# Expert up products with the weights stationary: weights copied inside SBUF for each slot, the turns of the product rows left out

## The reference, cut to what matters

```
D, F, E = 128, 512, 8                       # channels, hidden width, experts
logits = x @ gate_w
mult, sel = _sparse_mixer_routing(logits)   # two experts for each token, and their weights
w = jnp.sum(mult[:, :, None] * (sel[:, :, None] == jnp.arange(E)[None, None, :]), axis=1)
h = jax.nn.silu(jnp.einsum('th,ehf->etf', x, w1)) * jnp.einsum('th,ehf->etf', x, w3)
out = jnp.einsum('etf,efh,te->th', h, w2, w)
```

## Time and profile before

| what | us |
|---|---|
| median of 3 runs (1183.71 to 1185.48) | 1183.82 |
| the profiled execution | 1184.85 |
| its span, from the first to the last instruction | 1183.1 |
| TensorE busy (82% of the span) | 964.7 |
| DVE busy (68%) | 808.8 |
| ScalarE busy (43%) | 510.1 |
| GpSimd busy (36%) | 431.0 |
| DMA queue of SP, share of 16 DMA engines over the span | 13.5% |

### The profile page before, as it was taken

How to read it: one execution, slowest core, us unless ns; L and a number is a source line. 1 busy time by engine, 2 the same in 40 slices (tenths; PEclk the granted TensorE clock), 3 DMA queues, 4 the chain that set the end, 5 groups by cost and what they waited for, 6 DMA issues and landing times. The chain is left out here.

```text
span 1183.1 us, 17682 instructions
## 1 busy us (share of the span) xinstructions
PE 964.7 (82%) x6003; PEld 495.9 (42%) x6003; DVE 808.8 (68%) x1504; ACT 510.1 (43%) x1048; POOL 431.0 (36%) x506
## 2 busy tenths in 40 slices
PE   5497899999999999769867964599983994399993
PEld 3232322322222332346644423366651664156662
DVE  6886989999888770388987976533347786733335
ACT  5344577687877677432012111133334431123333
POOL 3320110011011111236853871266642785146661
PEclk9598999999999899979978996699996997689997
DMA  5843500000000000332101201011112210111114
GB/s 126 176 93 55 108 2 1 1 2 2 1 2 1 2 3 1 137 94 70 40 0 32 68 9 36 15 44 42 43 35 80 63 37 1 38 32 43 43 43 121
DMA packets 50205, 51.47 MB, mean 44 GB/s; under 512 B 7668, under 2 KB 39804, under 8 KB 50108
## 3 DMA queue, kind: packets, MB, share of 16 engines
q1 hardware_dynamic: 45128, 40.11, 13.5%
q0 software_dynamic: 4992, 10.23, 3.2%
HBM read 33.22 MB, written 16.91 MB: 42 GB/s over the span
## 5 line engine op out<-in xcount | busy, mean ns | idle before, releaser
L724 DVE TENSOR_REDUCE mpart<-ps 128x2 f32<-128x1024 f32 (+3 forms) x320 | 324.8, 1061 | 47.6 <-PE ps L775 29.2
L852 ACT ACTIVATE arena<-ps 128x512 f32<-128x512 f32 (+3 forms) x640 | 291.7, 543 | 132.1 <-PE ps L792 131.6
L792 PE MATMUL ps<-arena 51*128 51x512 bf16 (+3 forms) x640 | 175.2, 357 | 13.2 <-DMA arena<-mrow 6.3
L806 PE MATMUL ps<-arena,w 128*32 128x512 f32 (+3 forms) x1280 | 153.4, 551 | 2.8 <-ACT arena L852 2.1
L775 PE MATMUL ps<-arena 51*128 51x512 bf16 (+3 forms) x640 | 141.5, 361 | 12.1 <-DVE mpart L724 5.8
L694 POOL TENSOR_SCALAR_AFFINE_SELECT arena<-arena 128x512 f32<-128x512 f32 x64 | 40.6, 635 | 299.3 <-ACT arena L852 219.9
L1689 ACT ACTIVATE arena<-ps 128x512 f32<-128x512 f32 x78 | 46.6, 597 | 219.4 <-PE ps L1752 161.0
L1096 POOL TENSOR_TENSOR arena<-arena 128x512 f32<-128x512 f32 x96 | 121.0, 1272 | 46.2 <-DVE arena L1148 45.8
L1599 DVE COPY arena<-ps 128x128 f32<-128x128 f32 x78 | 22.8, 292 | 150.6 <-PE ps L1742 137.5
L792 PEld LDWEIGHTS ps<-arena 51*128 51x128 bf16 x640 | 49.3, 94 | 167.5 <-ACT arena L852 130.4
L1148 DVE TENSOR_TENSOR_SCAN arena<-ps,arena 128x512 f32<-128x512 f32 x96 | 118.3, 1253 | 0.4 <-POOL arena L1101 0.4
(11 more groups left out here) (265 smaller groups left out, 1440.5 us busy)
## 6 DMA issues: line engine op xcount, KB each, us to landing
w<-in_w SPq DMA_DIRECT2D x2, 2048.0 KB, 11.0
arena<-results SPq DMA_DIRECT2D x16, 256.0 KB, 5.1
arena<-q_stack SPq DMA_DIRECT2D x8, 384.0 KB
arena<-k_stack SPq DMA_DIRECT2D x8, 384.0 KB
arena<-g_v SPq DMA_DIRECT2D x9, 256.0 KB, 4.5
arena<-r_v SPq DMA_DIRECT2D x9, 256.0 KB, 3.6
arena<-l_v SPq DMA_DIRECT2D x9, 256.0 KB, 3.6
tokens<-arena SPq DMA_DIRECT2D x8, 256.0 KB, 2.4
```

The costliest lines, as they stand in the source:

```text
L724: nc.vector.tensor_reduce(out=mpart[:, 2 * pl:2 * pl + 2, t, kc], in_=ps[:, bank:bank + 2, 0:width], axis=AX.X, op=ALU.max).then_inc(ring_ ...
L792: nc.tensor.matmul(ps[:, n % ST, off:CH], rows(Ks, j % 2, 2 * g + j // 2, kt * P, (kt + 1) * P), rows(Qs, j % 2, 2 * g + j // 2, c * CH + ...
L806: ins = nc.tensor.matmul(ps[32 * j:32 * j + 32, O, off:CH], vg[kt // (NT // 2)][:, kt % (NT // 2), g * GH + j, :], probs[:, u % 2, j, off: ...
L852: nc.scalar.activation(probs[:, n % 2, j[0], off:CH], ps[:, (GH * n + j[0]) % ST, off:CH], ACT.Exp, scale=float(HD) ** -0.5).then_inc(exp_ ...
```

## The change

The up products change their sides: the expert's w1 and w3 become the stationary operand, in pieces of 128 hidden channels, and the turned tokens the moving one, 128 columns. Eight products take the place of two. Their result has the hidden channels on the partitions already, so the four turns on TensorE and the copy on ScalarE go, with the buffer `hid` and two semaphores; DVE's multiplication writes `hidT` itself. The down product of a slot moves one pass of the loop earlier.

The stationary pieces are read from a fixed place, `w13` (two buffers of 128 x 2 x 512). SP fills it: for each slot it reads the expert into a register, waits until the up products two slots back are done, and issues two DMAs of 128 x 512 words from `w1` and `w3` in SBUF to `w13` in SBUF. TensorE waits for both.

```
+            w13 = take(2 * 2 * F).rearrange("p (b u f) -> p b u f", b=2, u=2)
 ...
                             dve.wait_ge(silu_out, i + 1)
                             if i >= 2:
-                                dve.wait_ge(hid_turned, i - 1)
-                            nc.vector.tensor_tensor(hid[:, i % 2, :], ps[:, 2 + i % 2, :], act_a[:, i % 2, :],
-                                                    ALU.mult).then_inc(hid_ready, 1)
-                        s = i - 2
+                                dve.wait_ge(down_ready, i - 1)
+                            nc.vector.tensor_tensor(hidT[:, i % 2, :, :].rearrange("p f t -> p (f t)"), ps[:, 2 + i % 2, :],
+                                                    act_a[:, i % 2, :], ALU.mult).then_inc(hid_ready, 1)
+                        s = i - 1
 ...
                                      xnt[:, g * TPC:(g + 1) * TPC, :]).then_inc(stored_tokens, 16)
+
+                    sp.wait_ge(moe_loaded, 48)
+                    sp.wait_ge(expert_known, 1)
+                    for i in range(ST):
+                        expert = sp.value_load(expert_of[0:1, i:i + 1], min_val=0, max_val=E - 1)
+                        if i >= 2:
+                            sp.wait_ge(up_ready, i - 1)
+                        for u, weights in enumerate((w1, w3)):
+                            sp.dma_start(w13[:, i % 2, u, :], weights[:, expert, :]).then_inc(w_loaded[i % 2], 16)
 ...
                         if s >= 0:
-                            act.wait_ge(hid_turned, s + 1)
-                            if s >= 2:
-                                act.wait_ge(down_ready, s - 1)
-                            nc.scalar.copy(hidT[:, s % 2, :, :].rearrange("p f t -> p (f t)"), ps[:, 4 + s % 2, :]).then_inc(hidT_ready, 1)
 ...
-                            nc.tensor.matmul(ps[:, i % 2, :], xsT[:, i % 2, :], w1[:, expert[i], :], start=True, stop=True)
-                            nc.tensor.matmul(ps[:, 2 + i % 2, :], xsT[:, i % 2, :], w3[:, expert[i], :],
-                                             start=True, stop=True).then_inc(up_ready, 1)
-                        s = i - 1
-                        if 0 <= s < ST:
-                            pe.wait_ge(hid_ready, s + 1)
-                            if s >= 2:
-                                pe.wait_ge(hidT_ready, s - 1)
-                            for f in range(NF):
-                                ins = nc.tensor.transpose(ps[:, 4 + s % 2, f * P:(f + 1) * P], hid[:, s % 2, f * P:(f + 1) * P], ident)
-                            ins.then_inc(hid_turned, 1)
+                            pe.wait_ge(w_loaded[i % 2], 16 * 2 * (i // 2 + 1))
+                            for u in (0, 1):
+                                for f in range(NF):
+                                    ins = nc.tensor.matmul(ps[:, 2 * u + i % 2, f * P:(f + 1) * P], w13[:, i % 2, u, f * P:(f + 1) * P],
+                                                           xsT[:, i % 2, :], start=True, stop=True)
+                            ins.then_inc(up_ready, 1)
                         if i + 1 < ST:
                             turn_x(i + 1)
-                        s = i - 2
+                        s = i - 1
                         if s >= 0:
-                            pe.wait_ge(hidT_ready, s + 1)
+                            pe.wait_ge(hid_ready, s + 1)
```

More of the change, by code:

```diff
@@ L1458, in experts @@
             act_a = take(2 * F).rearrange("p (b f) -> p b f", b=2)
-            hid = take(2 * F).rearrange("p (b f) -> p b f", b=2)
             hidT = take(2 * F).rearrange("p (b f t) -> p b f t", b=2, f=NF)
+            w13 = take(2 * 2 * F).rearrange("p (b u f) -> p b u f", b=2, u=2)
             YB = 7
@@ L1469, in experts @@
             who_ready, holders_found, rows_known = (sem(f"{name}_{n}") for n in ("who_ready", "holders_found", "rows_known"))
-            stored_tokens, x_turned, xsT_ready, up_ready, silu_out, hid_ready, hid_turned, hidT_ready, down_ready, y_ready = (
-                sem(f"{name}_{n}") for n in ("stored_tokens", "x_turned", "xsT_ready", "up_ready", "silu_out", "hid_ready",
-                                             "hid_turned", "hidT_ready", "down_ready", "y_ready"))
+            stored_tokens, x_turned, xsT_ready, up_ready, silu_out, hid_ready, down_ready, y_ready = (
+                sem(f"{name}_{n}") for n in ("stored_tokens", "x_turned", "xsT_ready", "up_ready", "silu_out",
+                                             "hid_ready", "down_ready", "y_ready"))
+            w_loaded = [sem(f"{name}_w_loaded{b}") for b in (0, 1)]
             gathered = [sem(f"{name}_gathered{i}") for i in range(AHEAD)]
@@ L1601, in _ @@
                     take_turned(0)
-                    for i in range(ST + 2):
+                    for i in range(ST + 1):
                         if i + 1 < ST:
@@ L1683, in _ @@
                     norm.scalar(act)
-                    for i in range(ST + 1):
-                        if i < ST:
-                            act.wait_ge(up_ready, i + 1)
-                            if i >= 2:
-                                act.wait_ge(hid_ready, i - 1)
-                            nc.scalar.activation(act_a[:, i % 2, :], ps[:, i % 2, :], ACT.Silu).then_inc(silu_out, 1)
-                        s = i - 1
-                        if s >= 0:
-                            act.wait_ge(hid_turned, s + 1)
-                            if s >= 2:
-                                act.wait_ge(down_ready, s - 1)
-                            nc.scalar.copy(hidT[:, s % 2, :, :].rearrange("p f t -> p (f t)"), ps[:, 4 + s % 2, :]).then_inc(hidT_ready, 1)
+                    for i in range(ST):
+                        act.wait_ge(up_ready, i + 1)
+                        if i >= 2:
+                            act.wait_ge(hid_ready, i - 1)
+                        nc.scalar.activation(act_a[:, i % 2, :], ps[:, i % 2, :], ACT.Silu).then_inc(silu_out, 1)
                     for k in (1, 2):
```

## The result

The changed kernel is slower: 1226.58 us against 1183.76 (medians of four runs each), a ratio of 1.037 (95% interval 1.035 to 1.039). The forecast was 1154.0, the range ended at 1185. The profiled execution took 1224.57 us, its span is 1222.7. Lines have moved: L1758 are the up products, L1746 the turn of the tokens, L1769 the down product, L1601 DVE's copy of the turned tokens, L1618 its copy of the down product, L1699 Silu, L1656 and L1645 GpSimd's scatter and gather.

A forecast was written before the change was run, and what follows sets the result against it. TensorE's own work was taken to bound the slot loops. Per stage 12.9 us (35 slots) + 0.57 (head) + 1.63 (tail) = 15.1, both 30.2; 1184.85 - 30.2 + 0.4 = 1155.05, median 1.03 lower: 1154.0 us, range 1147 to 1185.

The forecast's parts named there:

- The matmuls: TensorE's slot: 16 short passes take 1.79 us, weight loads hidden, four turns (0.44) go; slot 2.79 us, 0.368 less.
- Head and tail: Ends of each stage's slot loop: head 9.65 us, 0.57 less; tail 5.74 us, 1.63 less.
- The 0.2 us a stage for the loads at the loop's start: Loop start: first four loads run beside the first gather, delaying TensorE 0 to 0.5 us; 0.2 taken in each stage.
- The sum: Whole kernel: 1184.85 - 30.2 + 0.4 = 1155.05 us; median of runs 1.03 lower, so 1154.0 us.
- The landing of the loads: SP's w13 loads in each slot: landed in 3.0 us with 3.5 free, so hidden, half a microsecond to spare.
- the first rival: Loads mildly late: at 4.0 us a load the slot is 3.03, 17 us back, 1171 us; chance 0.14.
- GpSimd ... has 0.2 us to spare and would be the next bound: GpSimd in the slot loop: scatter, gather and two gaps take at least 2.56 us of the 2.79 us slot.
- The rival in which GpSimd becomes the bound: Slot loop: GpSimd or TensorE's queue keeps the slot near 3.16 us, 1184 us; chance 0.04 for both together.
- TensorE's queue ... hands them over too slowly: Up products: 32 instructions where 8 were, handed over too slowly; slot near 3.16 us, 1184; chance 0.04, shared with GpSimd bound.
- The wait also lets TensorE's clock fall: Slot loop: late loads drop TensorE to half clock, slot 5.58 us, 195 us more, 1349 us; chance 0.03.
- What else goes ... Nothing.: Other engines' slot work: ScalarE's copy goes, DVE's wait changes, 1.53 us of Silu and product stay covered; no time change.

The follow-up runs named there:

- run without loads and gathers: The changed kernel without SP's loads (up products take a fixed expert's pieces) and without the loop's gathers (later slots reuse tokens of slots 0 to 5): 1152.04 us.
- after: The changed kernel with nothing left out, against the kernel before: 1226.58 us against 1183.76, ratio 1.037.
- short passes: The kernel before with each up product cut into four of 128 moving columns, no loads by SP: 1220.83 us.
- the best whole one: The changed kernel with three buffers of w13, one slot more between TensorE's steps and gathers ten slots ahead instead of six: 1195.52 us, ratio 1.012.
- one slot more of cover: The changed kernel with three w13 buffers and one slot more between TensorE's steps: 1215.46 us; with gathers ten slots ahead, 1195.52 us.
- no loads: The changed kernel without SP's loads of w13 and TensorE's wait for them; up products take a fixed expert's pieces: 1206.56 us.
- half the gathers: The changed kernel without the loads (a fixed expert's pieces) and with a gather in only every second slot of the loop: 1169.97 us.

## Why the prediction was wrong

- **The matmuls: right.** In the run without loads and gathers a slot is 2.79 us (turn of slot 3 at 1029.01 to that of slot 38 at 1126.63: 97.62 / 35), the 16 passes stand 0.1117 apart and their loads are hidden. By the sentence of the Trainium skill, "TensorE: Matmul & The Clock Gate", Part 3 (what overlaps and what doesn't), that the prediction cites, the full-row weight loads would lie open; this trace has 25 of them in every slot beside a TensorE that never idles, so the measurement decides against that sentence here.
- **Head and tail: right within 0.8 us without the loads, too short with them.** In the run without loads and gathers, first up product to the turn of slot 3: 8.82 us (9.65 forecast; the clock rose earlier). Turn of slot 38 to the end: 5.64 (5.74). But the head of m1 lasts 11.74 in after: the second up product starts 5.20 us behind the first, not 4.46, and still runs at the lower clock, 3.57 us to the turn behind it where the sum has 2.40. The 0.2 us a stage for the loads at the loop's start was too small there.

```profile
1054.29 3.78 PE L1758 MATMUL ps<-arena 128*128 128x128 f32 x16 [0.39 <-issue]
1059.49 3.78 PE L1758 MATMUL ps<-arena 128*128 128x128 f32 x16 [1.20 <-DVE arena L1601]
1066.03 0.27 PE L1746 MATMUL ps<-cst,arena 128*128 128x128 f32 x1
```

- **The sum, loads and gathers apart: right.** 1152.04 against 1154.0 less the 0.4 that stood for the loads at the loops' start, 1153.6.
- **The landing of the loads: right in the steady slot, wrong in some.** In after SP was released at 1081.84, and the last packet had landed at 1084.96: 3.1 us, where I took 3.0 and had 3.5 free. But SP needs 0.49 and 0.53 us for its two DMAs, where I had 0.33, so the half microsecond to spare was less, and where an instruction packet came it was gone. Without gathers the loads made 18.9 us, with the heads, and 1170.9 in all. That this is the first rival's time (1171) is luck: it had every load late by 0.5 us, and here the heads are longer and one load in four or five is late.
- **"GpSimd ... has 0.2 us to spare and would be the next bound": the step that failed.** I priced the scatter and the gather by their records and the gaps, 2.56 us, and took an engine with 0.2 us to spare for one that harms nobody. The gathers cost 54.5 us. GpSimd was not late with a scatter or a gather; while it issues them in a row, the signals of TensorE stand still. The rival in which GpSimd becomes the bound left the slot at 3.16 us and the time at 1184. The slot of after is 3.76 us in m0 and 3.78 in m1 (turn of slot 3 to that of slot 38, over 35).
- **"TensorE's queue ... hands them over too slowly": the nearest rival, with the wrong end.** It capped the loss at 3.16 us a slot, since the eight passes of L1770 keep 0.1117. So do the 16 (TensorE's issue was never slow); it is their completion that is told late, and that has no cap at the old slot.
- **"The wait also lets TensorE's clock fall": came in part, behind holds.** The rival had a chance of 0.03 and asked for late loads. The clock fell seven times for 3.4 us, up to 12 us of the time (estimate above).
- **"What else goes ... Nothing."** The cover for the copy of the turned tokens is the down product, 0.89 us, before and after. It was enough while the signals came in 0.04 us. Holds of 0.4 us could be seen in the trace of before, and the prediction read only TensorE's own row, which had no gap. The holds of after, up to 2.6 us, are longer than that cover.

**What stays open.** Shown is: without the gathers no holds, but for one of 0.3 us (with or without loads); more and longer holds with a shorter slot, more gathers, short passes, SP's loads, SP's register loads. What GpSimd's transfers share with the instructions of the other engines isn't shown. Every run here carries a granted clock and so was recorded while it ran; whether an execution that nobody records has the holds, these runs can't tell. No version tried beats the kernel before: the best whole one is 1195.5.

## What to carry to other kernels

Before making one long instruction into many short ones, look at what GpSimd does meanwhile: an engine whose records leave 0.2 us free is no cover, and a signal that comes 0.4 us late on a path with slack is a sign of what comes when the path has none. Look in the trace of before for instructions that start later than their producer's end while their engine is free, in all engines, not only in the one that is the bound. And price an edit by an undoing run for each of its parts: here they added up to 1225.4 of 1226.6 us.

## What the runs showed of the hardware that I had not expected

- TensorE's signals can come late, by up to 2.6 us in after and 5.0 us with one slot more of cover, in a burst (three within 0.13 us), while GpSimd issues scatters and gathers 1.28 us apart. Most come 1.6 to 1.9 us after the start of the last one where there are no loads (before, no loads, half the gathers, short passes) and 2.0 to 2.2 us after it where there are (after, one slot more of cover).
- A lone scatter every 2.79 us holds nothing: 0 of 161 signals, among them those of the up products and of the turn, due 1.0 and 1.1 us behind its start.
- In the slot at 1081.84 of after two DMAs of 256 KB from SBUF to SBUF landed 3.1 us after the wait before them was released, with packets of 2 KB of some 0.09 us; each issue kept SP 0.49 to 0.53 us.
- Six register loads a slot on an engine that nobody waits for cost the kernel before 17 us (1201.8 against 1184.7 measured beside it); its two loops are 19 us longer.
